# One swap transfer for q and k together in the two rope attentions

## The reference, cut to what matters

```
even, odd = jnp.split(x, 2, axis=-1)
rope = jnp.concatenate([even * cos - odd * sin, even * sin + odd * cos], axis=-1)
s = einsum('bihd,bjhd->bhij', rope(q), rope(k)) / D_HEAD   # causal mask, softmax, times v, times w_ao
```

## Time and profile before

| What | Value |
|---|---|
| Median of 3 runs | 1799.9 us (1792.04 to 1802.42) |
| Profiled execution, its time | 1790.62 us |
| Profiled execution, its span | 1788.2 us |
| Busy: PE, DVE, ACT, POOL | 91%, 58%, 57%, 43% of the span |
| Mean granted TensorE clock | 0.971 |
| Swap transfers, `heads=1` | 128 of 128 KB |
| Swap transfers, `heads=2` | 256 of 64 KB |

### The profile page before, as it was taken

The page is one execution under the profiler, slowest core; times in us unless marked ns, Lnnn a source line. Parts: engine busy times, 40 slices in busy tenths (PEclk is TensorE's granted clock), DMA queues, the critical chain, the costliest instruction groups (busy, mean ns, idle before and its releaser), DMA issues. The chain is left out here.

```text
span 1788.2 us, 27849 instructions
## 1 busy us (share of the span) xinstructions
PE 1633.5 (91%) x8911; PEld 1063.8 (59%) x8929; DVE 1037.2 (58%) x2511; ACT 1017.0 (57%) x2184; POOL 767.5 (43%) x715
## 2 busy tenths in 40 slices
PE   5899998896997999999889999999989999978998
PEld 3567653353895666666455555555448887434786
DVE  5856675630224655555456666666558887662675
ACT  4534555542423555555556666666538887754786
POOL 1235533117252566666266555655324442122363
PEclk8999998998999999999999999999989999989999
DMA  1008231001114222222121111111036652000330
GB/s 42 2 18 194 55 123 82 1 1 42 65 44 127 59 59 60 59 59 59 60 55 41 48 47 39 47 48 41 20 109 236 224 216 98 4 0 22 140 114 24
DMA packets 61865, 124.67 MB, mean 70 GB/s; under 512 B 14258, under 2 KB 29477, under 8 KB 55228
## 3 DMA queue, kind: packets, MB, share of 16 engines
q1 hardware_dynamic: 59580, 119.24, 22.7%
q0 software_dynamic: 2144, 3.70, 0.7%
HBM read 79.05 MB, written 11.02 MB: 50 GB/s over the span
## 5 line engine op out<-in xcount | busy, mean ns | idle before, releaser
L1992 ACT ACTIVATE h_probs<-psum,h_nmax 128x512 f32<-128x512 f32 (+3 forms) x256 | 133.2, 526 | 119.0 <-DVE h_nmax L2073 64.0
L2073 DVE CUSTOM_DVE_ANT_0 psum<-psum,h_mask 128x512 f32<-128x512 f32 (+3 forms) x256 | 122.7, 510 | 83.3 <-PE psum L1876 80.3
L917 ACT ACTIVATE psum<-psum,f_b 128x512 f32<-128x512 f32 x200 | 132.3, 662 | 30.0 <-PE psum L874 30.0
L1804 POOL TENSOR_TENSOR h_swapped<-h_swapped,rope_tables 128x512 f32<-128x512 f32 x64 | 81.8, 1279 | 152.8 <-DMA h_swapped<-h_raw 152.6
L840 POOL TENSOR_TENSOR e_lo<-e_gated,e_hi 128x512 fp32r<-128x512 f32 x59 | 76.0, 1288 | 147.8 <-ACT e_hi L929 147.8
L1992 ACT ACTIVATE a_probs<-psum,a_nmax 128x512 f32<-128x512 f32 (+3 forms) x128 | 67.5, 528 | 121.4 <-DVE a_nmax L2073 73.6
L1804 POOL TENSOR_TENSOR a_swapped<-a_swapped,a2f_a_tables 128x512 f32<-128x512 f32 x64 | 83.2, 1300 | 122.8 <-DMA a_swapped<-a_raw 122.7
L952 DVE TENSOR_TENSOR e_lo<-psum,e_hi 128x512 fp32r<-128x512 f32 x168 | 114.8, 683 | 25.3 <-ACT psum L917 25.3
L126 PE MATMUL psum<-rope_tables,mean_w 128*128 128x256 f32 x490 | 121.5, 398 | 7.3 <-ACT h_raw L1982 2.8
L1883 PEld LDWEIGHTS psum<-ident,h_probs 128*128 128x128 f32 x640 | 71.4, 141 | 80.4 <-issue 52.8
L1883 PE MATMUL psum<-ident,h_probs 128*128 128x128 f32 x640 | 115.1, 287 | 1.7 <-ACT h_probs L1992 1.4
(11 more groups left out here) (496 smaller groups left out, 4124.5 us busy)
## 6 DMA issues: line engine op xcount, KB each, us to landing
e_gate<-gates SPq DMA_DIRECT2D x39, 1024.0 KB, 4.6
a_swapped<-a_raw SPq DMA_DIRECT2D x128, 128.0 KB, 2.3
h_swapped<-h_raw SPq DMA_DIRECT2D x256, 64.0 KB, 2.0
e_gate<-gates SPq DMA_DIRECT2D x16, 512.0 KB, 7.2
f_w<-in_l_experts SPq DMA_DIRECT2D x32, 128.0 KB, 4.6
slots<-a_empty SPq DMA_DIRECT2D x1, 2600.0 KB
f_w<-in_l_experts SPq DMA_DIRECT2D x9, 256.0 KB, 4.9
e_got<-slots SPq DMA_DIRECT2D x7, 325.0 KB, 5.4
```

The costliest lines, as they stand in the source:

```text
L917: nc.scalar.activation(to, hidden_bank(n), ex.act_func, **bias(n)).then_inc(act_ready, 1)
L1804: nc.gpsimd.tensor_tensor(swapped[:, j, :], swapped[:, j, :], tables[:, 2 * j + 1, :], ALU.mult).then_inc(sin_ready, 1)
L1992: nc.scalar.activation(probs[:, j % 4, 0:(q + 1) * P], ring[j % RING][:, 0:(q + 1) * P], ACT.Exp, scale=-1.0, bias=nmax[:, j % 8:j % 8 + 1 ...
L2073: nc.vector.tensor_tensor_reduce(s, s, mask[:, (QT - 1 - q) * P:], scale=-1.0, scalar=-SENT, op0=ALU.add, op1=ALU.min, accum_out=nmax[:, j ...
```

## The change

SP issues the swaps of q and k of a unit together: for each half one transfer that covers both, `[64, 2, 512]` or `[32, 2, 512]`. It therefore waits for both `raw` tiles and for both adds of the unit before. Transfers per unit go from 4 to 2 with `heads=1` and from 8 to 4 with `heads=2`; the bytes stay. One semaphore takes the place of two, and POOL and ACT wait for all transfers of the unit where they waited for those of q or of k alone.

```diff
-        swap_loaded = [st.sem(f"{n}_swapped") for n in "qk"]
+        swap_loaded = st.sem("swapped")
...
                 for V in range(NU):
-                    for j in range(2):
-                        sp.wait_ge(raw_ready[j], V + 1)
-                        if V >= 1:
-                            sp.wait_ge(qk_ready, 2 * V - 1 + j)
-                        for lo, hi in halves:
-                            sp.dma_start(swapped[hi:hi + half, j, :], raw[lo:lo + half, j, :]).then_inc(swap_loaded[j], 16)
+                    sp.wait_ge(raw_ready[0], V + 1)
+                    sp.wait_ge(raw_ready[1], V + 1)
+                    if V >= 1:
+                        sp.wait_ge(qk_ready, 2 * V)
+                    for lo, hi in halves:
+                        sp.dma_start(swapped[hi:hi + half, :, :], raw[lo:lo + half, :, :]).then_inc(swap_loaded, 16)
...
-                        pool.wait_ge(swap_loaded[j], (V + 1) * (16 * len(halves)))
+                        pool.wait_ge(swap_loaded, (V + 1) * (16 * len(halves)))
...
                     if V >= 1:
-                        act.wait_ge(swap_loaded[j], V * (16 * len(halves)))
+                        act.wait_ge(swap_loaded, V * (16 * len(halves)))
```

## The result

The changed kernel takes 1823.84 us (median of 4 runs, 1817.98 to 1825.24) against 1801.16 us of the kernel before (4 runs, 1792.04 to 1802.61): a ratio of 1.0131, 95% interval 1.009 to 1.0171. That is 22.7 us slower, where 9.2 were forecast. The profiled execution took 1824.2 us (span 1822.4, mean granted clock 0.967).

A forecast was written before the change was run, and what follows sets the result against it. PE bounds both attentions, but in heads=1 the swap loop of 9.33 us exceeds the 8.97 us unit. Steady heads=1 7.9, its start -0.1, heads=2 +1.4: 9.2 us on 1799.9 gives 1809 us, whole range 1796 to 1820.

The forecast's parts named there:

- The loop: Steady heads=1: POOL's work, SP's issue and the swaps' landing no longer overlap across units; 9.33 us against 8.97.
- L = 1.7 + 2.38 = 4.08 us; I take 4.05: Heads=1 swaps, first issue to last landing: 1.7 us independent of size plus 2.38 us of data at 221 GB/s.
- the mild form of the rival of later landings: Larger transfers land much later, both loops bind: 5.5 us, 1844 us in all; mild form 4.4 us, 1817; chance 0.08.
- The slack of 0.7 us: Steady heads=1: lateness absorbed before PE waits at line 1916, from the third or fourth late unit on; 0.7 us deducted.
- the forecast's 8.6 us: Steady heads=1: lag growing by 0.36 us per unit for 24 units, 8.6 us, before the slack is deducted.
- Start of heads=1: Chain to the first scores: POOL starts 1.7 us later, DVE's cosines save 1.1 and 0.7; together -0.1 us.
- DVE's two savings: Start of heads=1: cosine of unit 1 takes 0.68 instead of 1.81 us (-1.1); PE's wait at 588.57 goes (-0.7).
- Heads=2: Steady loop of 10.6 us fits the unit of 12.08, cost 0; at the start +0.8 and 0.5, together +1.4 us.
- The 0.5 for unit 1: Start of heads=2: POOL's later cosine of unit 1 delays ACT's overwriting of `raw`; 0 to 0.9 us, taken as 0.5.
- later starts change TensorE's clock: Both attentions' starts: named as a sign of being wrong, if later starts change TensorE's granted clock; no size given.
- POOL and DVE hindrance: Heads=1 rival: late adds and `widen` meet DVE's cosines, up to 0.5 us a unit, 12 more, 1821 us; chance 0.06.
- Hidden rival: Larger transfers run faster, 370 GB/s; heads=1 loop of 8.4 us stays under 8.97, nothing in steady part, 1800 us; chance 0.2.

The follow-up runs named there:

- e3: The changed kernel with two buffers of `swapped`, SP waiting for the adds two units back: 1803.45 us, ratio 1.0022 to the kernel before.
- e11: The changed kernel with one more POOL copy of 128x512 per unit, ahead of k's multiplication: 1853.55 us, ratio 1.028 to the kernel before.
- e4: The kernel before with the change in the heads=1 attention alone: 1819.48 us, ratio 1.0098.
- e6: The changed kernel with four transfers of 32 partitions in heads=1, each for q and k together, same waits: 1826.59 us, ratio 1.0126 to the kernel before.
- e5: The kernel before with the change in the heads=2 attention alone: 1796.79 us, ratio 0.9983.
- e1: The changed kernel, all its waits kept, with four (eight) small transfers per unit as before: 1875.14 us, ratio 1.0411 to the kernel before.

## Why the prediction was off

The mechanism was right. One term of the sum was too small, one was missing, and smaller ones were off.

- **The loop.** It binds as described: POOL 5.20 forecast, 5.21 measured; handover 0.06, 0.09; PE waits at line 1916; e3 and e11 show it from both sides, by taking the buffer out and by lengthening it.
- **The step that failed: "L = 1.7 + 2.38 = 4.08 us; I take 4.05".** Measured 4.29 to 4.30. The data were no slower but faster, 2.25 us. The part that doesn't depend on size, 1.7 us from a landing of 128 KB, was 2.05: 1.0 ahead of the first byte and 1.0 behind the last. The loop is 9.60 instead of 9.33, 24 x 0.27 = 6.5 us more. The excess over PE's 8.97 was a difference of two near numbers: an error of 6% in L made it 0.63 instead of 0.36. This is nearly the mild form of the rival of later landings (L = 4.4, +16), which I had given little; its reason, longer landings of larger transfers, is what the tail shows.
- **The missing term: disturbances that the loop passes on.** The forecast gave all 24 units the ordinary length. Of the 24, 8 hold a packet of instruction queue q8 between k's add and the landing, and these are the ones with waits of 4.48 to 5.54 us (5.21, 5.54, 4.48, 4.51, 5.17, 5.53, 5.25, 4.79). All 16 others wait 4.37 to 4.40, also the two that hold only a packet of the other instruction queue (q14, some 8 KB). The longer waits make 5.4 us. In the unit behind each of the three longest, k's add takes 1.59 to 1.82 us instead of 1.27, 1.2 us in all. Together these are the 236.95 - 24 x 9.60 = 6.5 us. Eight packets of q8 fall into the 24 steady units of the kernel before as well, but only two of its periods stand out, 9.24 and 9.39 us, and the next ones make them up (8.68, 8.54): its slack takes up what a late landing costs. e4 has the same units long by the same amounts, and the seven late landings of e6 hold such a packet too, though one packet there goes with no delay. This rests on coincidence and on the late packets shown above; no run took the loads away, so that the loads are the cause is argued, not shown.
- **The slack of 0.7 us.** It was used up ahead of the units that the forecast counted. Counted from the first `raw`, POOL's first multiplication of unit 7 is already 2.9 us late, and PE's output at the same time only 0.4. PE waits at line 1916 from the first counted unit on (0.3 us between 641 and 651 us), not from the third or fourth. So the forecast's 8.6 us stand without the deduction: 7.9 + 0.7 + 6.5 + 6.5 = 21.6 us, against 21.8 in POOL's marks. PE loses 22.9 us from the output of unit 4 to that of unit 29, one unit more.
- **Start of heads=1.** -0.1 forecast, +0.4 at PE's outputs of units 0 to 4. DVE's two savings came as forecast; but POOL starts 5.80 us after the beginning of unit 0's `raw` instead of 3.66, +2.1 where +1.7 was forecast (L again).
- **Heads=2.** Steady 0, right (12.09, 12.09). Start +1.4 forecast (its two parts, 0.8 and 0.5, make 1.3), +2.3 at PE in the trace: 1.0 from the later swap, where 0.8 was forecast, and 1.3 in the stretch of lower granted clock. The 0.5 for unit 1 didn't come. One of the prediction's own signs of being wrong, that later starts change TensorE's clock, came true here, in small. In the time of e5 nothing of it appears.
- **POOL and DVE hindrance.** It exists, and costs less than its rival said: the copy at line 1788 takes 1.07 us instead of 0.61 in this stretch (median of 22), and DVE's pair of cosines up to 1.96 instead of 1.28. But the copy is outside the loop, so it only adds to PE's wait at line 1916. e11 shows what it costs once it falls on k's add in every unit, 0.37 us each, and e3 what it costs where PE sets the pace, some 0.12.
- **Hidden rival.** It needed data at 265 GB/s or more and L under 3.69. The data ran at 0.524 MB in 2.25 us, 233 GB/s, and L was 4.3.

The Trainium skill (SBUF — State Buffer, section "Can I just issue two DMAs to hit both halves?") says that two concurrent DMAs on the two halves of the partitions give only some 6% over a single one. The same page of the Trainium skill, section "Door 1: The DMA port swizzle", puts the limit of a single one at about 218 GB/s. The traces fit that: 233 GB/s with both swaps, 213 for the single store from 32 partitions. The same page of the Trainium skill, section "SBUF: two separate sides", says that a VectorE instruction with two SBUF inputs and a GpSimd one that reads SBUF lock a shared port pair, and that the later one waits until the first has finished. The trace agrees as far as it goes. In the changed kernel the cosines start first (705.01) and line 1788's copy, from 705.36, is longer by 0.46 us. In e3 the copy starts first (702.61) and keeps its 0.61 us, and the cosines, from 702.91, are longer by 0.18.

## What to carry to other kernels

Joining transfers also joins their waits: write out the loop from the last read of the buffer, through issue and landing, to the next read, and compare it with the period of the engine that bounds. When the two are near each other, an error of some per cent in one term decides the result. Here a second buffer took back 19 of 23 us, and none of the three shapes of transfer brought the loop under the period. Halving the issues paid only where all of them were waited for together (e1, `heads=2`), and it was no substitute for the overlap. A loop without slack also passes on every late landing that was absorbed before. And where an engine's marks run at the loop's pace, read the loss from the engine that bounds: POOL's marks in `heads=1` show a lateness of 2.9 us by unit 7, PE's outputs 0.4.

## What I had not expected of the hardware

- Two 256 KB swaps move their 512 KB faster than four of 128 KB (2.25 against 2.5 us in e6) and yet land no sooner: from the last byte to POOL's start 1.0 against 0.6 us.
- In the changed kernel, every swap with a packet of some 16 KB of the instruction queue q8 among its data lands 0.1 to 1.15 us late (in e6 seven of eight do); in the one shown, single packets arrive behind the rest.
- 4.6 us of idle PE ahead of the first scores went along with some 4 us more in the first units behind them, with a granted clock of 0.52 in the first 10 us. At the start of `heads=2`, a start 1.0 us later went along with 1.3 us more in filler and first scores, at 0.69 instead of 0.88.
